# Layer 1's second part: expert projections in four chunks of 512 tokens, the first of them inside the last two halves of the attention

## What is computed

```python
xn = _layernorm(x, axis=-1)
s = _L1_attn_ref(xn, ...)            # 16 heads of 8, causal, softmax, then y @ W_O.T
# _L1_ffn_ref(xn, ...):
n1 = _layernorm(x, ln1_w, ln1_b)
rw = _gating(n1, smha_sim, smha_gates, 2)          # (token, 8 experts)
q = jnp.einsum('btc,ech,bte->bth', n1, q_proj, rw)
k = jnp.einsum('btc,ech,bte->bth', n1, k_proj, rw)
v = jnp.einsum('btc,ech,bte->bth', n1, v_proj, rw)
# causal attention of one head per batch over q, k, v
attn_out = jnp.einsum('bth,ehc,bte->btc', attn, o_proj, rw)
hs = x + attn_out
# then a second norm and gating, 8 experts with gelu, hs + moe_out
```

## Time and profile before

| | |
|---|---|
| median of 3 runs (lowest, highest) | 1267.21 us (1263.99 to 1267.85) |
| the profiled execution | 1270.17 us |
| its span, first to last instruction | 1268.4 us |
| mean granted TensorE clock | 0.902 |
| PE busy, share of the span | 1108.5 us, 87% |
| DVE / ACT / POOL busy | 811.1 / 645.1 / 193.0 us |
| end of layer 1's attention | 992.6 us |
| last unit of the projections done | 1081.8 us |

### The profile page before, as it was taken

The page is one execution under the profiler, slowest core; times in us unless marked ns, Lnnn a source line. Parts: engine busy times, 40 slices in busy tenths (PEclk is TensorE's granted clock), DMA queues, the critical chain, the costliest instruction groups (busy, mean ns, idle before and its releaser), DMA issues.

```text
span 1268.4 us, 19558 instructions
## 1 busy us (share of the span) xinstructions
PE 1108.5 (87%) x7308; PEld 522.8 (41%) x7308; DVE 811.1 (64%) x1599; ACT 645.1 (51%) x1241; POOL 193.0 (15%) x313
## 2 busy tenths in 40 slices
PE   6499999699999999999875699899998899897777
PEld 4366666222222222222232344344442567553444
DVE  6633333498898898888367487787870435556654
ACT  4322222127787787778731356567776322433434
POOL 2145655000111010010000001112321000001000
PEclk9799999759999999999976579789997699898888
DMA  4612223311122201100025003211223300000331
GB/s 120 209 47 91 91 91 70 96 26 36 36 51 61 55 20 36 38 18 10 19 84 166 27 28 81 76 45 43 91 86 94 109 1 1 1 1 0 134 135 33
DMA packets 62182, 77.79 MB, mean 61 GB/s; under 512 B 15804, under 2 KB 40076, under 8 KB 60044
## 3 DMA queue, kind: packets, MB, share of 16 engines
q1 hardware_dynamic: 53592, 66.39, 16.8%
q10 hardware_dynamic: 8500, 10.21, 2.9%
HBM read 61.32 MB, written 14.61 MB: 60 GB/s over the span
## 4 chain that ended last, share of the span: by engine, by line
PE 65%; DVE 19%; ACT 8%; SPq 3%; issue 3%; DMA 2%; ACTq 0%; POOL 0%; DVEq 0%
PE PS L1624 62%; DVE mx L1388 10%; ACT arena L919 5%; SPq L566 2%; SPq L574 1%; DMA arena<-drev_dram 1%; PE PS L1637 1%; DVE arena L1202 1%; DVE arena L1205 1%; DVE arena L1598 1%; PE PS L2035 0%; DMA arena<-mrow 0%; DVE arena L1166 0%; DVE small L1584 0%; DVE arena L1154 0%
## 5 line engine op out<-in xcount | busy, mean ns | idle before, releaser
L1624 PE MATMUL PS<-arena 128*32 128x512 f32 (+13 forms) x3656 | 615.2, 489 | 75.3 <-DVE mx L1388 21.0
L1388 DVE TENSOR_REDUCE mx<-PS 128x1 f32<-128x512 f32 (+3 forms) x896 | 500.3, 624 | 98.0 <-PE PS L1624 97.6
L919 ACT ACTIVATE arena<-PS 128x512 f32<-128x512 f32 (+3 forms) x896 | 436.4, 556 | 229.5 <-PE PS L1624 222.2
L1624 PEld LDWEIGHTS PS<-arena 128*32 128x32 f32 (+3 forms) x3656 | 159.4, 105 | 447.8 <-DVE mx L1388 173.6
L1624 PE MATMUL PS<-x_hi,w_hi_lo 128*128 128x512 f32 x320 | 145.1, 495 | 0.8 <-DVE combT L1266 0.4
L1492 DVE TENSOR_TENSOR fw<-PS,fw 128x512 f32<-128x512 f32 x80 | 55.3, 692 | 119.7 <-ACT fw L971 117.9
L971 ACT ACTIVATE fw<-PS 128x512 f32<-128x512 f32 x80 | 47.8, 597 | 123.5 <-PE PS L1624 123.4
L843 POOL TENSOR_TENSOR fw<-fw,arena 128x512 f32<-128x512 f32 x64 | 84.9, 1326 | 88.9 <-DVE fw L1492 88.9
L1624 PE MATMUL PS<-fw 128*128 128x512 f32 (+3 forms) x184 | 90.3, 578 | 0.0
L795 POOL TENSOR_TENSOR arena<-arena,fw 128x512 f32<-128x512 f32 x31 | 39.7, 1279 | 270.3 <-DMA fw<-sum_dram 270.3
L1624 PE MATMUL PS<-arena,fw 128*128 128x512 f32 x128 | 69.8, 666 | 5.2 <-DVE arena L1580 5.2
(11 more groups left out here) (307 smaller groups left out, 1081.6 us busy)
## 6 DMA issues: line engine op xcount, KB each, us to landing
arena<-comb_dram SPq DMA_DIRECT2D x16, 1024.0 KB, 5.2
arena<-comb_dram SPq DMA_DIRECT2D x16, 512.0 KB, 7.3
fw<-sum_dram SPq DMA_DIRECT2D x31, 256.0 KB
q_dram<-arena SPq DMA_DIRECT2D x24, 256.0 KB, 3.6
k_dram<-arena SPq DMA_DIRECT2D x24, 256.0 KB, 3.8
arena<-drev_dram SPq DMA_DIRECT2D x32, 192.0 KB, 4.2
arena<-k_dram ACTq DMA_DIRECT2D x20, 204.0 KB
fw<-in_ffn_w SPq DMA_DIRECT2D x10, 384.0 KB, 3.1
```

The lines of the kernel that those rows point to most:

```text
L919: s.activation(Pr[:, m % 8, 0:w], bank(4 + m % 3, 0, w), ACT.Exp).then_inc(A["e_done"], 1)
L1388: v.reduce_max(mx[:, H % 2, kh, n:n + 1], bank(U % RING, 0, w), axis=AX.X, negate=True).then_inc(A["ring_free"], 1)
L1624: return nc.tensor.matmul(out_, lhsT, rhs, start=start, stop=stop)
```

## The change

The projections go by chunks of 512 tokens: 32 units x of nine matmuls, x // 8 the chunk and x % 8 the expert. Chunk n collects in banks 0 to 2 if n is even and in 4 to 6 if it is odd. Units 0 to 7 stand within the last steps of the attention (table TAIL: the four steps of half 14 and the eight of half 15): DVE makes the weighted input from step TAIL[0] on, ACT the upper part after the exponentials of step TAIL[x], and PE has unit x two steps later, q, k and v behind heads 0, 1 and 3. Their inputs lie in a tile of their own, xe_hi_lo, with two slots; later units have four slots in e_hi_lo. Output projections 0 and 1 follow straight after the attention, 2 and 3 before unit 16, in banks 3 and 7; the value transposes of batch 0 stand before unit 18 and use these banks too, and those of batch 1 follow the second scores. A chunk's copies out of PSUM stand among the units of the next. Slot 9 of SP loads rows 0 and 4, slot 11 row 5, slot 14 nothing; the first halves of rows 6 and 7 are issued by ACT at the start of half 14, the second halves by SP after the attention.

```diff
-PROJECT = 5
+TAIL = [(HALVES - 2, i) for i in range(4)] + [(HALVES - 1, i) for i in range(8)]
...
-        Xe = [at(72, 4), at(76, 4)]
-        Xe_r = [e_hi_lo[:, h * TOK:(h + 1) * TOK].rearrange("p (s t) -> p s t", s=2) for h in range(2)]
+        Xe = [at(72, 2), at(74, 2)]
+        Xe_first = [xe_hi_lo[:, 1024 * h:1024 * (h + 1)].rearrange("p (s t) -> p s t", s=2) for h in range(2)]
+        Xe_later = [e_hi_lo[:, h * TOK:(h + 1) * TOK].rearrange("p (s t) -> p s t", s=4) for h in range(2)]
...
+        def wait_unit_used(eng, x):
+
+            if 2 <= x < EXP:
+                eng.wait_ge(x_used, x - 1)
+            if x >= EXP + 4:
+                eng.wait_ge(x_used, x - 3)
...
             attention_feed(1, {
-                8: comb_out, 9: lambda: rw_behind(7, 0), 10: lambda: rw_behind(7, 1), 11: lambda: rw_behind(7, 4),
-                12: lambda: rw_behind(11, 2), 13: lambda: rw_behind(11, 3), 14: lambda: rw_behind(7, 5)})
+                8: comb_out, 9: lambda: rw_behind(7, 0, 4), 10: lambda: rw_behind(7, 1), 11: lambda: rw_behind(7, 5),
+                12: lambda: rw_behind(11, 2), 13: lambda: rw_behind(11, 3)})
...
+                        if l == 1 and (H, i) in TAIL[:EXP]:
+                            upper_part(TAIL.index((H, i)))
...
+            def upper_part(x):
+                act.wait_ge(x_made, x + 1)
+                wait_unit_used(act, x)
+                s.activation(unit_x(x)[0], Xe[x % 2], ACT.Copy).then_inc(ehi_made, 1)
...
+            def last_rows():
+
+                act.wait_ge(comb_stored, 32)
+                act.wait_ge(att[1]["st_ps"], HG * steps_before(1, HALVES - 2))
+                rows = comb_dram[1].rearrange("(e t) k -> e (t k)", e=EXP)
+                for e in (6, 7):
+                    act.dma_start(rwb[e][:, 0:SEQ], rows[e, 0:SEQ].partition_broadcast(P)).then_inc(rw_in[e], 16)
...
+            for x in range(EXP, NC * EXP):
+                upper_part(x)
+                if x in (EXP, EXP + 1):
+                    projected(x - EXP)
+                if x == EXP + 1:
+                    second_qv(0)
+                if x == 2 * EXP + 1:
+                    projected(2)
+                    projected(3)
+                    second_qv(1)
+            second_qv(2)
+            second_qv(3)
...
+            def unit(x, end):
+
+                if x < end:
+                    if x == 0:
+                        dve.wait_ge(att[1]["av_done"], steps_before(1, HALVES - 2))
+                    if x >= 2:
+                        dve.wait_ge(elo_made, x - 1)
+                    unit_rows(dve, x)
+                    tok = chunk(x // EXP)
+                    v.tensor_tensor(Xe[x % 2], n1T[:, tok], rwb[x % EXP][:, tok], ALU.mult).then_inc(x_made, 1)
+                if x >= 1 and x != EXP or x == end:
+                    hi, lo = unit_x(x - 1)
+                    dve.wait_ge(ehi_made, x)
+                    v.tensor_tensor(lo, Xe[(x - 1) % 2], hi, ALU.subtract).then_inc(elo_made, 1)
...
+                            if l == 1 and (H, i) in TAIL[2:EXP + 2] and j != 2:
+                                expert_unit(TAIL.index((H, i)) - 2, {0: (0,), 1: (1,), 3: (2,)}[j])
...
+            def expert_unit(x, projections=range(3)):
+
+                n, e = x // EXP, x % EXP
+                if 0 in projections:
+                    if x == 0:
+                        pe.wait_ge(ew_split, 12)
+                        pe.wait_ge(att[1]["ring_free"], n_units[1])
+                    pe.wait_ge(elo_made, x + 1)
+                for p in projections:
+                    ins = split_mm(bank(4 * (n % 2) + p), [w_e_hi[p][:, e, :], w_e_lo[p][:, e, :]], unit_x(x),
+                                   start=e == 0, stop=e == EXP - 1)
+                if 2 in projections:
+                    ins.then_inc(x_used, 1)
...
+            for x in range(EXP, NC * EXP):
+                if x == EXP:
+                    project_out(1, 0, bank(3))
+                    pe.wait_ge(att[1]["o_ev"], HALVES)
+                    project_out(1, 1, bank(7))
+                    pe.wait_ge(att[1]["e_done"], HG * steps_before(1, HALVES))
+                if x == 2 * EXP:
+                    pe.wait_ge(att[1]["pj_ev"], 1)
+                    project_out(1, 2, bank(3))
+                    pe.wait_ge(att[1]["pj_ev"], 2)
+                    project_out(1, 3, bank(7))
+                    pe.wait_ge(x_ev, 2)
+                    pe.wait_ge(vt_ev, 1)
+                if x == 2 * EXP + 2:
+                    pe.wait_ge(x_ev, 4)
+                    pe.wait_ge(att[1]["pj_ev"], NC)
+                    value_transposes(0)
+                if x == 3 * EXP:
+                    pe.wait_ge(vt_ev, 2)
+                expert_unit(x)
...
-            pe.wait_ge(x_ev, 8)
-            pe.wait_ge(vt_ev, 6)
+            pe.wait_ge(x_ev, 6)
+            pe.wait_ge(vt_ev, 5)
             for i in range(STEPS):
                 if i < TILES:
                     scores(i)
-                if i == 0:
+                if i == 1:
+                    pe.wait_ge(x_ev, 8)
+                    pe.wait_ge(vt_ev, 6)
                     value_transposes(1)
```

More of the change, by code:

```diff
@@ L288, in block_net @@
             x_lo = part("x_lo", 8)
-            part("below_e", 48, F32)
+            part("below_xe", 32, F32)
+            xe_hi_lo = part("xe_hi_lo", 8)
+            part("below_e", 8, F32)
             e_hi_lo = part("e_hi_lo", 16)
@@ L474, in chunk, with value_bank, unit_x, unit_rows @@
             return slice(512 * n, 512 * (n + 1))
+        def value_bank(b, c):
+            return bank((3, 7)[c] if b == 0 else 6 + c)
+        def unit_x(x):
+            return [(Xe_first[h][:, x % 2, :] if x < EXP else Xe_later[h][:, x % 4, :]) for h in range(2)]
+        def wait_unit_used(eng, x):
[3 more added lines that the diff above has]
+                eng.wait_ge(x_used, x - 3)
+        def unit_rows(eng, x):
+            eng.wait_ge(rw_in[x % EXP], 32 if x % EXP >= 6 and x >= 2 * EXP else 16)
         def ffn_experts(eng, expert, chain=None, per=0):
@@ L1038, in projected, with second_qv @@
                     act.wait_ge(att[1]["v_staged"], GROUPS)
[L1039 to L1052, removed]
-                    s.activation(Xe_r[0][:, e % 2, :], Xe[e % 2], ACT.Copy).then_inc(ehi_made, 1)
-                    if b == 0 and e in (PROJECT, PROJECT + 1):
-                        for c in (2 * (e - PROJECT), 2 * (e - PROJECT) + 1):
-                            projected(c)
-                    if b == 1 and e == 0:
-                        second_qv(0)
-            second_qv(1)
+                s.activation(sT1[:, 512 * c:512 * (c + 1)], bank((3, 7)[c % 2]), ACT.Copy).then_inc(att[1]["pj_ev"], 1)
+            def second_qv(n):
+                b, c, first = n // 2, n % 2, 4 * (n % 2)
+                act.wait_ge(x_used, EXP * (n + 1))
+                s.activation(qT[b][:, chunk(c)], bank(first), ACT.Copy, scale=1.0 / math.sqrt(C)).then_inc(x_ev, 1)
+                s.activation(vT[b][:, chunk(c)], bank(first + 2), ACT.Copy).then_inc(x_ev, 1)
+            for x in range(EXP, NC * EXP):
[10 more added lines that the diff above has]
+            second_qv(3)
             def chain(b, plan, n):
@@ L1423, in attention @@
                         sequence(unit_plan[l][H][i])
+                        if l == 1 and (H, i) in TAIL[:EXP + 1]:
+                            unit(TAIL.index((H, i)), EXP)
                         if H >= 1 and i == sum_step(l, H):
@@ L1547, in values_back, with second_k @@
                     dve.wait_ge(vt_ps, b * 2 + c + 1)
[L1548 removed]
+                    v.tensor_copy(vtok[b][:, 4 * c:4 * c + 4, :].rearrange("p k c -> p (k c)"), value_bank(b, c)).then_inc(vt_ev, 1)
             dve.wait_ge(att[1]["av_done"], steps_before(1, HALVES))
[L1551 to L1570 removed]
+            def second_k(n):
+                dve.wait_ge(x_used, EXP * (n + 1))
+                v.tensor_copy(kT[n // 2][:, chunk(n % 2)], bank(4 * (n % 2) + 1)).then_inc(vt_ev, 1)
+            for x in range(EXP, NC * EXP + 1):
+                unit(x, NC * EXP)
+                if x == EXP + 1:
+                    invert_sums(HALVES - 1)
+                if x == EXP + 2:
+                    dve.wait_ge(att[1]["pj_ps"], 2)
                     second_k(0)
[L1572 removed]
+                if x == 2 * EXP + 2:
+                    second_k(1)
+                if x == 2 * EXP + 4:
                     values_back(0)
[L1574 removed]
+            second_k(2)
+            second_k(3)
             for i in range(STEPS):
@@ L1982, in value_transposes @@
                     for k in range(4):
[L1983 removed]
+                        ins = nc.tensor.transpose(value_bank(b, c)[:, P * k:P * (k + 1)], vT[b][:, (4 * c + k) * P:(4 * c + k + 1) * P], ident[:, :])
                     ins.then_inc(vt_ps, 1)
[L1986 to L2007 removed]
```

59 lines of the change are left out of this document (10 added, 49 removed).

## The result

| | before | changed |
|---|---|---|
| median of 4 runs (lowest, highest) | 1266.38 us (1263.99 to 1267.85) | 1248.33 us (1245.75 to 1252.63) |
| the profiled execution, and its span | 1270.17, 1268.4 us | 1247.89, 1246.1 us |
| mean granted TensorE clock | 0.902 | 0.919 |

The ratio is 0.9877 (95% interval 0.9834 to 0.9921): 18.05 us faster, where 25.6 were forecast. The two profiled executions lie 22.3 us apart. 4.45 of these are not the change's: 2.40 had built up before DVE's reciprocal of half 9 (908.23 in the earlier trace rows, 905.83 now), and 2.05 come after the first transpose of the scores, both in stretches whose instructions the change left almost as they were. So I compare stretches within a profile, from the first exponentials of half 14 to the first transpose of the scores: 1089.50 - 957.30 = 132.2 us before, 1069.25 - 954.90 = 114.35 now, 17.85 less.

A forecast was written before the change was run, and what follows sets the result against it. PE was taken as the bound: its work, clock and holes. 35.0 + 63.7 + 3.9 = 102.6 us against 128.2, 25.6 less, from the median 1267.21 gives 1241.6, say 1242; range 1237 to 1251.

The forecast's parts named there:

- Part 1: Halves 14 and 15 from 961.30 us: PE's 17.1 attention, 16.3 units and 1.6 hand-overs make 35.0 us.
- Part 2: From step (14, 2) on, new matmuls fill the places where PE was short of work, so the clock stays 1.00.
- the other case: Clock stays down at 0.50 to the end of the attention: +31.2 us, 1273, slower by 0.4%; chance 0.05.
- falls for a while: Clock at 0.50 for 7 to 14 us in thin or last steps costs 3.5 to 7, about 1247; chance 0.15.
- Part 3: ACT within the halves: 2.7 us a step against PE's about 3.8, so covered by PE, cost 0.
- ACT bounds: Strict order on ACT makes six steps of the halves about 4.6 instead of 3.8 us: +5, 1247; chance 0.14.
- Part 4: Moved row loads on ACT's and SP's queues cost 0; at worst sums 3 us late, row 3 +1 to +2.
- Parts 5 to 7: After the attention: the 3.71 us hole and 2.9 us lost clock go; then projections 63.7 us, into scores 3.9.
- the rest of the projections: After the attention: 24 units 49.0 us, two output projections 13.8, value transposes 0.9; sum 63.7 us, no waits for copies.
- Into the scores: Last unit to first transpose: 7.7 us less 2.1 of wait for copies and 1.7 of clock leaves 3.9 us.

The follow-up runs named there:

- all-behind run: The changed kernel with units 0 to 7 behind the attention instead of within it, all else kept: 1257.9 us, ratio 0.9932.
- first all-rows run: The changed kernel with energies of the last two halves made from an identity matrix over 128 rows, masks still 64 rows: 1248.23 us, ratio 0.9869.
- one-block kernel: The changed kernel with each unit's nine matmuls in one piece behind head 3, instead of three pieces: 1242.96 us, ratio 0.9832.
- the stream: TensorE alone, the whole computation left out, repeated matmul groups: three f32r matmuls took 0.68 us, behind one bf16 matmul of 51 rows 1.21 us.

## Why the prediction was right and wrong

- *Part 1, PE's work within the two halves: the step that failed.* The units' 2.04 us and the clock were right. What was mis-sized is the term "I add 1.6 us, 0.2 for each of eight steps, for hand-overs between the two kinds of work". Each step has three such meetings, each a pair of mode changes at 0.3 us: 24 x 0.31 = 7.4 us. The attention ended 11.9 us later instead of 3.7. Of these 8.2 us, 5.8 (7.4 - 1.6) are this term by the rows, and 5.6 came back when the small matmuls had 128 rows. A second step failed without being written down: the attention's own work was taken as unchanged, 1.85 us a full step, and that includes two energies side by side, which the pieces keep apart. At 0.22 us in each of eight steps an estimate of it is 1.8 us. The remaining 0.6 us stay open.
- *Part 2, the clock.* 1.00 throughout, as forecast; the all-behind run shows the other case. But it is not sure: it fell for 6 to 14 us in the profiles of four related kernels. The rival "falls for a while" is real, and was not the cause here.
- *Part 3, ACT.* Right: it waited for PE. The rival "ACT bounds" gave nearly the right time, 1247, by the wrong mechanism; it became true only when the energies stood four in a row.
- *Part 4, DMA issues.* Right at 0: the reciprocal of half 9 shows no wait on its sums, and PE none on unit 2. DVE did wait, 1.82 us at 962.64, for the row of unit 3; PE needed that unit two steps later, and lost nothing.
- *Parts 5 to 7.* Right: 63.7 us forecast for the rest of the projections; from the last product's start to the last unit's end are 64.3, of which the product itself takes 0.36 (the output projections start at 1001.73), so 64.0. Into the scores 3.9 forecast, 3.6 measured. No hole.

The sum over the stretch was 25.6 less, and is 17.85. The median, 1248.33, lies inside the range of 1237 to 1251, but outside the 1238 to 1246 that went with the sum. The range went up to 1251 to take in two rivals, ACT as the limit and a fall of the clock, and neither happened. That it holds the measured time is luck as far as the mechanism goes.

## What to carry to other kernels

Before putting small matmuls among large ones on TensorE, count the places where a shape of up to 64 rows, or of 32 output partitions, meets one over the whole array, and price each meeting, there and back, at 0.3 us: three projections spread over a step cost 0.9 us of changes for 2.04 us of work, in one block 0.3. See also which small matmuls go side by side in different rows, and don't part them; that was 0.2 us more in each step. Put a unit in one piece, but where the consumer of the small results has enough banks to go on with; here the order behind head 3 (1242.96 us) beat the kernel before, and by the steps (4.13 against 4.95 us) the change. If an experiment leaves the total where it was, look at its steps: in the first all-rows run the saving was there, and a nearly equal cost had appeared next to it.

## What the runs showed of the hardware

- A pair of mode changes costs 0.3 us at the full clock: 1.21 against 0.93 us for four matmuls of 512 columns.
- Energies in rows 0 to 50 and in rows 64 to 114, written one behind the other, run side by side: two cost 0.22 us, as much as one (one-block kernel against the change). Two matmuls that both use rows 0 to 50 took 0.43 us in the stream.
- 96 and 115 rows behave as 128 (0.93 us a group); 32, 51 and 64 rows do not (1.21).
- The same instructions in the same order ran at 1.00 in one execution and at 0.51 for 14 us in another, with PE busy all the time. To know the clock of a kernel, one profile is not enough.
